# Graph convolution on one core: the extremes of the destinations in sixteen pieces, one behind each feature copy

## The reference, cut to what matters

```
f = x @ W1 (two irreps), feat = first half, self = second half
e = feat[src]                                  # a gather of 412,500 rows of 128 floats
h = gelu(gelu(edge_attr_8 @ W_mlp1) @ W_mlp2);  w = h @ Wp
mid = products of w, e and edge_attr_4          # 256 numbers per edge
n = segment_sum(mid, dst) ;  conv = n @ W2
y = cos(mix) * self + sin(mix) * conv
out = layernorm(x + y)
```

## Time and profile before

| what | us |
|---|---|
| runs shown, median of 3 | 4148.26 (4148.19 to 4149.33) |
| profiled execution | 4149.65 |
| its span in the profile | 4147.7 |
| POOL busy / idle before its gathers | 3053.3 / 1031.0 |
| DVE busy | 2873.0 |
| PE busy | 3362.1 |

### The profile page before, as it was taken

The page is one execution under the profiler, slowest core; times in us unless marked ns, Lnnn a source line. Parts: engine busy times, 40 slices in busy tenths (PEclk is TensorE's granted clock), DMA queues, the critical chain, the costliest instruction groups (busy, mean ns, idle before and its releaser), DMA issues.

```text
span 4147.7 us, 39164 instructions
## 1 busy us (share of the span) xinstructions
PE 3362.1 (81%) x12559; PEld 2149.7 (52%) x12559; DVE 2873.0 (69%) x3921; ACT 704.2 (17%) x1437; POOL 3053.3 (74%) x3255
## 2 busy tenths in 40 slices
PE   8888888888888787888878888788888888887886
PEld 5555555555555555555545555555555555555554
DVE  4876766666667676677676766767667666676676
ACT  4111111111111111111111111111111111111114
POOL 4777777777777777777777777777777777777773
PEclk9999999999999999999999999999999999999997
DMA  5222222222222222222222222222222222222222
GB/s 176 57 58 61 57 57 61 57 57 61 57 57 57 61 57 57 61 57 57 62 57 57 57 61 57 57 61 57 57 61 57 57 57 62 57 57 60 54 54 84
DMA packets 215288, 255.98 MB, mean 62 GB/s; under 512 B 135075, under 2 KB 161055, under 8 KB 213519
## 3 DMA queue, kind: packets, MB, share of 16 engines
q0 software_dynamic: 103584, 211.46, 19.7%
q1 hardware_dynamic: 110072, 43.99, 4.0%
q10 hardware_dynamic: 1600, 0.17, 0.0%
HBM read 242.59 MB, written 12.80 MB: 62 GB/s over the span
## 4 chain that ended last, share of the span: by engine, by line
POOL 72%; issue 24%; PE 2%; ACT 1%; DVE 1%; POOLq 0%; DMA 0%; ACTq 0%; DVEq 0%
POOL gath L424 72%; ACT big L572 1%; PE weights L638 1%; PE bank L713 0%; PE weights L652 0%; PE bank L625 0%; POOLq L447 0%; PE bank L666 0%; POOLq L446 0%; PE bank L672 0%; DVE base_f L872 0%; DVE relmax L871 0%; PE weights L702 0%; POOLq L443 0%; DVE stats L1004 0%
## 5 line engine op out<-in xcount | busy, mean ns | idle before, releaser
L424 POOL DMA_INDIRECT gath<-feature_table,idx x3223 | 3041.2, 944 | 1031.0 <-issue 1030.7
L702 PE MATMUL weights<-wpbd,big 128*128 128x256 f32 x3224 | 991.0, 450 | 600.4 <-DVE big L952 348.2
L702 PEld LDWEIGHTS weights<-wpbd,big 128*128 128x128 f32 x3224 | 698.3, 222 | 1046.2 <-DVE big L952 432.0
L938 DVE TENSOR_TENSOR weights<-weights,gath 128x512 f32<-128x512 f32 x403 | 281.6, 699 | 896.4 <-DMA gath<-feature_table,idx 892.7
L713 PE MATMUL bank<-dst_rows,sel 128*80 128x256 f32 x3214 | 761.7, 398 | 0.4 <-ACT ztsb L526 0.4
L713 PE MATMUL bank<-big,sel 128*80 128x256 f32 x3232 | 743.2, 390 | 0.4 <-ACT ztsb L526 0.4
L510 ACT ACTIVATE h<-bank 128x512 f32<-128x512 f32 x400 | 238.8, 597 | 2950.0 <-PE bank L688 2950.0
L713 PEld LDWEIGHTS bank<-dst_rows,sel 128*80 128x80 f32 x3214 | 517.9, 161 | 244.4 <-issue 49.2
L713 PEld LDWEIGHTS bank<-big,sel 128*80 128x80 f32 x3232 | 505.0, 156 | 229.2 <-issue 27.1
L693 PE MATMUL bank<-h,w2bd 128*128 128x512 f32 x800 | 435.8, 626 | 137.9 <-ACT h L510 137.9
L923 DVE SCALAR_TENSOR_TENSOR sel<-dst_t,base_bc,bank 128x1280 f32<-128x1280 int32 x202 | 311.2, 1541 | 184.8 <-PE bank L713 183.5
(11 more groups left out here) (92 smaller groups left out, 1338.8 us busy)
## 6 DMA issues: line engine op xcount, KB each, us to landing
gath<-feature_table,idx POOLq DMA_INDIRECT x3223, 2.5
e<-in_edge_attr SPq DMA_DIRECT2D x50, 256.0 KB, 3.1
ea_t<-in_edge_attr SPq DMA_DIRECT2D x50, 128.0 KB, 2.3
feature_table<-gath SPq DMA_DIRECT2D x4, 1280.0 KB, 5.8
out<-big SPq DMA_DIRECT2D x4, 1280.0 KB
big<-in_x SPq DMA_DIRECT2D x3, 1280.0 KB, 10.9
idx<-in_src SPq DMA_DIRECT2D x50, 32.0 KB, 1.9
dst_t<-in_dst SPq DMA_DIRECT2D x50, 32.0 KB
```

The costliest lines, as they stand in the source:

```text
L424: pool.indirect_dma_start(out=gath[:, s % SLOTS, t, :], out_offset=None, in_=table[:, :], in_offset=bass.IndirectOffsetOnAxis(ap=idx[:, s, ...
L702: last = pe.matmul(wgt_ps[:, 512 * c + 256 * r:512 * c + 256 * (r + 1)], h2[:, s // SUPER % 2, s % SUPER, 2 * c + r, :], wpbd[:, :], start ...
L938: dve.tensor_tensor(w[:, :, 0:2, :], w[:, :, 0:2, :], f[:, :, 0, :].unsqueeze(2).to_broadcast([128, n, 2, MUL]), ALU.mult)
```

## The change

The four reductions over a whole row (128 partitions by 2048 int32) become sixteen over a quarter of a row (128 by 512). Each stands behind one feature copy, from batch 6 to batch 21: row 0 maximum and minimum of quarter 0, then of quarter 1, and so on. They go into a new tile `partial`. Behind the last one, two more reductions over `partial` (128 by 2 from 128 by 8) put together the row's maxima and minima, and the four small operations follow as before. PE's spreading of the bases moves from behind batch 8 to behind batch 23, DVE's reading of flag and bases from behind batch 10 to behind batch 24, the last. Line numbers of the changed kernel are 4 higher up to the copies, and 6 higher behind the extremes.

```
+        partial = sb("partial", [128, 2, BLOCK_ROWS, 4])
+        QUARTERS = 4
+        EXTREMES = 2 * BLOCK_ROWS * QUARTERS
...
-                if n == OFFSETS_FROM + BLOCK_ROWS:
+                if n == OFFSETS_FROM + EXTREMES + 1:
                     pe.wait_ge(s_ones, 1)
                     pe.wait_ge(s_diag, BLOCK_ROWS)
...
-            def extremes(c):
-                dve.tensor_reduce(relmax[:, c:c + 1], dst_i[:, c, :], AXIS_X, ALU.max)
-                dve.tensor_reduce(base_f[:, c:c + 1], dst_i[:, c, :], AXIS_X, ALU.min).then_inc(s_min, 1)
+            def extreme(i):
+                c, q, op = i // (2 * QUARTERS), i // 2 % QUARTERS, i % 2
+                dve.tensor_reduce(partial[:, op, c, q:q + 1], dst_i[:, c, BLOCK // QUARTERS * q:BLOCK // QUARTERS * (q + 1)],
+                                  AXIS_X, (ALU.max, ALU.min)[op]).then_inc(s_min, 1)
...
-                if OFFSETS_FROM <= n < OFFSETS_FROM + BLOCK_ROWS:
+                if OFFSETS_FROM <= n < OFFSETS_FROM + EXTREMES:
                     if n == OFFSETS_FROM:
                         dve.wait_ge(s_dst, 16 * DST_LOADS)
-                    extremes(n - OFFSETS_FROM)
-                if n == OFFSETS_FROM + BLOCK_ROWS - 1:
-                    dve.wait_ge(s_min, BLOCK_ROWS)
+                    extreme(n - OFFSETS_FROM)
+                if n == OFFSETS_FROM + EXTREMES - 1:
+                    dve.wait_ge(s_min, EXTREMES)
+                    dve.tensor_reduce(relmax[:, 0:BLOCK_ROWS], partial[:, 0, :, :], AXIS_X, ALU.max)
+                    link(dve.tensor_reduce(base_f[:, :], partial[:, 1, :, :], AXIS_X, ALU.min))
                     link(dve.tensor_tensor(relmax[:, 0:BLOCK_ROWS], relmax[:, 0:BLOCK_ROWS], base_f[:, :], ALU.subtract))
...
-                if n == OFFSETS_FROM + BLOCK_ROWS + 2:
+                if n == OFFSETS_FROM + EXTREMES + 2:
                     dve.wait_ge(s_small, 1)
```

More of the change, by code:

```diff
@@ L161, in build_program @@
         s_tab = [sem(f"table_stored{i}") for i in range(PIECE_SLOTS)]
-        s_min = sem("block_minimum_ready")
+        s_min = sem("partial_extremes_ready")
         s_ones = sem("ones_ready")
@@ L217, in build_program @@
         OFFSETS_FROM = 6
+        QUARTERS = 4
+        EXTREMES = 2 * BLOCK_ROWS * QUARTERS
+        assert OFFSETS_FROM + EXTREMES + 2 < NODE_BATCHES
         INIT = NODES // NODE_BATCHES
```

## The result

The changed kernel takes 4138.91 us, median of 12 runs (4138.02 to 4139.58), against 4148.54 for the kernel before (12 runs, 4148.17 to 4150.09). The ratio is 0.9976 with a 95% interval of 0.9968 to 0.9983, so it is 9.6 us faster. The forecast was 4138.0, in a range of 4136.7 to 4141.8.

What follows compares the result with a forecast made beforehand. POOL's gathers bound the kernel once begun, so only the first gather's start counts: 11.7 - 0.5 (load 4) - 0.5 (last copy) - 0.4 (piece 4) = 10.3 us gain, 4139.35, less 1.39 execution excess: 4138.0; range 4136.7 to 4141.8.

Steps and rivals of the forecast that it cites:

- What bounds it: Whole kernel: the end is the first gather's start (62.23 us) plus a constant; the change is worth what it moves that start.
- The cost per batch: DVE, per batch: a piece holds 0.60 us, a feature copy 0.61, together 1.21 against ACT's 1.40, so hidden.
- the second rival: DVE's pieces: the spare 0.19 us per batch is not there; time 4140.4 to 4142.8 us; chance 0.07.
- the fourth rival: Copies of batches 6 to 21: pieces holding DVE 1.43 us or more eat the gain; 4150.2 at 1.55; chance 0.05.
- The pause: Node stage: DVE's whole-row reductions leave PE dry at its two-deep banks; removing this gains 11.7 us.
- Load 4: Load of x for PE's batch 10 transpose: a new 0.6 us wait, costing 0.5 us, bounds 0 and 0.6.
- Load 5: Load of x needed at batch 15: lands at 29.7 us with 0.7 us to spare, cost nothing.
- Load 6: Load of x needed at batch 20: there at 36.9 us, wanted at 37.4, the thinnest case, cost nothing.
- The end of the stage: Last node batches: batch 22's copy 1.16 us late, PE's spreading 0.8 us, last copy 0.5 us late.
- The term of 0.4 us for piece 4: Table stores before the first gather: piece 5 waits behind the later piece 4, costing 0.4 us, bounds 0 and 1.0.
- The queue: DMA queue behind 28.6 us takes over: first gather at 55.1 us, gain 7.1, time 4141.2; chance 0.14.
- given back at block 4: Block 4's gathers: PE's edge stage does not move with them, so the gain is lost, time 4148; chance 0.04.

Runs made afterwards that it cites:

- tiny_pieces: The changed kernel with its sixteen reductions over two columns each in place of 512; 4138.73 us (0.9975).
- doubled: The changed kernel with each of the sixteen reductions done twice, the second into a tile nobody reads; 4144.60 us.
- halves: The changed kernel with eight 1024-column reductions in place of sixteen of 512, chain, spreading and reading following behind batches 13, 15 and 16; 4141.55 us.
- tiny_rows: The kernel before with its four reductions over two columns each, bases as early as before; 4138.83 us (0.9976).
- rows_chain_last_2: The same kernel as rows_chain_last, run again; 4145.70 us against 4149.05 for the kernel before (0.9992).
- chain_last: The changed kernel with DVE's small chain behind batch 24's copy, not 21's, and PE's spreading behind batch 24's multiply, not 23's; 4138.57 us (0.9974).
- after_2: The changed kernel, nothing altered, run once more beside rows_chain_last_2; 4139.00 us against 4149.05 for the kernel before (0.9976).
- loads_ahead: The changed kernel with loads 5 and 6 of x issued ahead of the stores of pieces 0 and 1; 4138.96 us (0.9976).
- rows_chain_last: The kernel before, whole-row reductions kept, with small chain, spreading and reading of bases all behind batch 24; 4956.86 us against 4954.85 (1.0004).

## Why the prediction was right

**What bounds it.** Right. Span less first gather is the same in twelve profiles within 1.3 us, while the first gather moves by up to 11.9, so the change is worth the shift of the first gather.

**The cost per batch.** Right. 0.676 us a piece in place of 0.68 and 0.60 us of hold; tiny_pieces shows it hidden, which answers the second rival, and doubled and halves show it on the path beyond the pace. That is the place and the price of the fourth rival: at doubled's 1.18 us of hold the kernel is still 4 us faster than before.

**The pause.** The size came out, and so did its source, DVE's hold; the way from there to PE was right only in part. The prediction had PE run dry at its banks. The kernels say: taking away the hold alone gives 9.9 us (tiny_rows), moving chain and bases alone 3.3 (rows_chain_last_2), both together 10.4 (chain_last, 4148.98 to 4138.57). The two gains overlap and can't be added: while the hold stands, 3.3 us of it reach PE by its wait in order for the base diagonal and by DVE's chain of 1.0 us, which wait would be short without the hold. It was visible before the run: PE's longest wait there was for `h`, not for features. In the prediction's own sum, 22.51 + 15 x 1.40 is 43.5 and not 43.6, which makes no difference.

**Load 4.** Predicted 0.6 us of wait, 0.53 found. It is no constant: 0.72 in after_2, 1.13 in tiny_pieces, none in loads_ahead, for PE comes to batch 10 earlier or later from run to run. **Load 5.** Predicted no wait; it landed 12.0 us after its issue at 18.46 in place of 10.9, and PE waited 0.35 us, which cost some 0.13 by loads_ahead. Together the two held ACT's copies up by 0.5 us: from batch 9 to batch 24 they took 21.59 us, and 21.10 in loads_ahead, where PE waits for neither. So the term of 0.5 came out for two waits in place of one. **Load 6** was in time: no wait for it in the profile.

**The end of the stage.** The copy of batch 22 came 1.16 us late, as forecast. The last copy came 0.56 us late: before, 56.66 follows the copy of batch 22 (54.52) by 2.1; after, 45.67 follows that of batch 21 by 4.11, where 1.41 + 2.14 would be 3.55. PE's spreading held it for 0.62 us (44.36 to 44.98), not 0.8. The term of 0.4 us for piece 4 was wrong: from the last copy's end to the first gather it is 5.10 us (46.16 to 51.26), and was 5.09. Flag and bases cost the first gather nothing.

**The mis-sized terms.** The sum gave 51.9 us for the first gather; the profiles show 51.26 and 51.40. Of the 0.6 us, 0.4 are the term for piece 4, and 0.3 are chance: ACT's copy of batch 3, ahead of every piece, already stood at 13.80 in place of 14.12. Yet 4138.0 is 0.9 us too low. The 11.7 us of pause were read from an execution that was itself 1.1 us over the median of twelve, and its excess was then taken off the result as well, as if it were outside the node stage. The profiled pair differs by 10.8 us, the medians by 9.6 and 10.05. The rest of that execution's span, 4085.5 us, is no longer than in the others, so its excess most likely lay in the node stage: an estimate from 4148.54 - 1.95 - 4085.6 puts a typical first gather of before near 61.0 us, and the pause about 1 us smaller than read. It stays an estimate, for there is one profile of the kernel before and the rest varies by 1.3 us between profiles. That the forecast was only 0.9 off is in part luck: it had the gain in one execution too small by 0.7 us and took off 1.39 us that were not there to take.

**The rivals.** The queue did not take over: the DMA share falls to 0.41 at 38 to 40 us, so it ran dry between pieces 2 and 3. Nothing was given back at block 4: POOL's idle time is issue but for 0.3 us. But more of the spare went than forecast. The sum of block 0 and the gather that would wait for it stand so in the changed kernel:

```profile
117.25 7.96 PE L717 MATMUL bank<-big,sel 128*80 128x256 f32 x32
131.24 0.94 POOL L428 DMA_INDIRECT gath<-feature_table,idx  x1 [0.30 <-issue]
```

The sum ends at 125.21, 7.2 us earlier than before, the gather starts 11.0 earlier, and the spare fell from 9.8 to 6.0 us. The prediction had 1.1 us of new delay. PE's edge stage began 9.84 us earlier (48.76 and 58.60), which is 1.15 of delay. The other 2.6 came right behind, while PE's granted clock was 0.50: four multiplies by `winit` take 3.54 us there and took 1.84 before.

```profile
49.66 3.54 PE L656 MATMUL weights<-acc,winit 128*128 128x500 f32 x4
```

## What to carry to other kernels

A long operation that nobody needs yet can be cut into pieces and dealt out behind the operations of a steady loop, and costs nothing as long as piece and loop operation together stay under the pace of the slowest engine; both are read from two rows, and the loss beyond is the excess times the number of pieces. Look as well for the in-order wait of another engine that hangs on its result: moving that wait alone gave 1.6 us here, and 3.3 with the small chain, without any cutting (by medians; the intervals of both include no change). Such gains overlap with that of the cut and are not to be added to it. A term read from one execution carries that execution's own excess; don't take the excess off a second time.

## What was not expected of the hardware

PE's granted clock fell to 0.50, 1.2 GHz, in the changed kernel when PE stood from about 45.7 to 48.76 us for flag and bases; in the kernel before, a pause of 1.97 us at the same place left it at 1.00. The length of the pause does not settle it: in tiny_rows one of 1.95 us was followed by 0.52 at 48 to 50 us. The first multiplies of the edge stage ran slower for it. The gathers did not wait for them, but it took 2.6 us of the spare at block 4.

The same kernel before took 4147.6 to 4150.7 us in four series of runs and 4947.7 to 4959.9 in a fifth, and the record gives that one the same chip number as the series of 4149 us that came six minutes later, so it isn't shown to belong to the chip. There POOL waited about 3.8 us a block for something that the profile doesn't name, and PE's mean clock was 0.849 in place of 0.927. POOL was not alone: in rows_chain_last, near 307 us, ACT, DVE and POOL go on within 1 us of each other, after 15.02, 8.40 and 3.89 us of idle time that the profile puts down to the same "remote". Two of these rows:

```profile
306.51 1.55 DVE L923 SCALAR_TENSOR_TENSOR sel<-dst_t,base_bc,bank 128x1280 f32<-128x1280 int32 x1 [8.40 <-remote]
306.55 0.60 ACT L510 ACTIVATE h<-bank 128x512 f32<-128x512 f32 x1 [15.02 <-remote]
```

The differences between kernels can't be read there: rows_chain_last lay 2 us over the kernel before, whose own runs spread over 12. The first gather of rows_chain_last stood 1 us later than that of its repeat (58.48 and 57.52), so the node stage ran there much as here. The cause was not tried.
